# Values of two key steps in one go behind every second step, in a causal two-softmax attention block

## What is computed

```python
scores = einsum('bhid,bhjd->bhij', q, k) / sqrt(hd)
std_out = out_proj(softmax(where(mask, scores, neg)))
gsa_scores = scores + position_sensitivity * splat_attn
gsa_out = out_proj(softmax(where(mask, gsa_scores, neg)))
return (1.0 - blend) * std_out + blend * gsa_out
# the layer
x = layernorm(x + attn(x)); x = layernorm(x + ffn(x))
```

## Time and profile before

| | us |
|---|---|
| median of 3 runs | 417.15 |
| lowest, highest | 415.52, 419.78 |
| the profiled execution | 420.38 |
| its span | 418.6 |

### The profile page before, as it was taken

The page is one execution under the profiler, slowest core; times in us unless marked ns, Lnnn a source line. Parts: engine busy times, 40 slices in busy tenths (PEclk is TensorE's granted clock), DMA queues, the critical chain, the costliest instruction groups (busy, mean ns, idle before and its releaser), DMA issues.

```text
span 418.6 us, 6705 instructions
## 1 busy us (share of the span) xinstructions
PE 392.4 (94%) x2234; PEld 258.5 (62%) x2234; DVE 314.3 (75%) x908; ACT 231.1 (55%) x451; POOL 112.0 (27%) x163
## 2 busy tenths in 40 slices
PE   8989886899999999999999999999887999999995
PEld 7656553566566566566565565556344578888884
DVE  2767744999979889889889789799302447999956
ACT  4964123156666667567567577677486756344100
POOL 8569100020221230230330320346557110000000
PEclk9999978699999999999999999999898999999999
DMA  6152664000044044053053056500000000000002
GB/s 201 36 99 45 102 103 74 1 3 2 3 78 78 4 78 76 6 89 65 6 96 59 7 97 144 215 2 1 3 2 0 2 2 0 0 1 2 2 0 100
DMA packets 12907, 19.69 MB, mean 47 GB/s; under 512 B 5493, under 2 KB 8565, under 8 KB 12873
## 3 DMA queue, kind: packets, MB, share of 16 engines
q1 hardware_dynamic: 10328, 18.18, 21.6%
q0 software_dynamic: 1536, 1.07, 1.5%
q10 hardware_dynamic: 1008, 0.02, 0.1%
HBM read 5.26 MB, written 1.05 MB: 15 GB/s over the span
## 4 chain that ended last, share of the span: by engine, by line
PE 80%; DVE 10%; ACT 6%; issue 2%; DMA 2%; SPq 1%; DVEq 0%; ACTq 0%
PE ps L931 19%; PE ps L905 17%; PE ps L870 16%; PE ps L834 7%; PE ps L736 5%; PE ps L738 5%; PE ps L737 5%; DVE ps L1225 4%; PE ps L892 2%; DMA x_sb<-_attn_hidden_states_dram 2%; ACT pr L684 1%; PE ps L798 1%; DVE mpart L1218 1%; PE ps L818 1%; ACT gauss L643 1%
## 5 line engine op out<-in xcount | busy, mean ns | idle before, releaser
L684 ACT ACTIVATE pr<-ps 128x512 f32<-128x512 f32 (+2 forms) x320 | 157.3, 561 | 82.3 <-PE ps L931 80.8
L1225 DVE CUSTOM_DVE_ANT_0 ps<-ps,causal 128x512 f32<-128x512 f32 (+3 forms) x256 | 145.6, 615 | 15.6 <-PE ps L870 13.8
L870 PE MATMUL ps<-k_st,q_st 65*128 65x512 f32 (+5 forms) x384 | 121.2, 368 | 9.9 <-DVE mpart L1225 6.4
L931 PE MATMUL ps<-q_st,k_st 67*128 67x512 f32 (+7 forms) x384 | 127.1, 374 | 0.0
L931 PEld LDWEIGHTS ps<-q_st,k_st 67*128 67x128 f32 (+1 forms) x384 | 68.4, 191 | 67.8 <-ACT pr L684 42.8
L870 PEld LDWEIGHTS ps<-k_st,q_st 65*128 65x128 f32 (+1 forms) x384 | 69.3, 194 | 26.2 <-DVE mpart L1225 13.7
L905 PE MATMUL ps<-pr,vx 128*32 128x512 f32 (+3 forms) x768 | 83.4, 507 | 1.1 <-ACT o_sb L670 1.1
L528 POOL TENSOR_SCALAR_AFFINE_SELECT pr<-pr 128x512 f32<-128x512 f32 x64 | 40.5, 633 | 115.2 <-ACT pr L684 115.2
L1218 DVE TENSOR_REDUCE mpart<-ps 128x2 f32<-128x256 f32 (+2 forms) x96 | 54.7, 596 | 6.7 <-PE ps L870 6.7
L1225 DVE DVE_READ_ACCUMULATOR2_ANT mpart<- 128x1 f32 x256 | 36.2, 141 | 0.0
L905 PEld LDWEIGHTS ps<-pr,vx 128*32 128x32 f32 x768 | 15.3, 108 | 23.6 <-ACT pr L684 14.6
(11 more groups left out here) (186 smaller groups left out, 511.6 us busy)
## 6 DMA issues: line engine op xcount, KB each, us to landing
q_st<-base_hiq SPq DMA_DIRECT2D x28, 64.0 KB
k_st<-base_hik SPq DMA_DIRECT2D x28, 64.0 KB
q_st<-feat_hiq SPq DMA_DIRECT2D x28, 64.0 KB
k_st<-feat_hik SPq DMA_DIRECT2D x28, 64.0 KB
x_sb<-_attn_hidden_states_dram SPq DMA_DIRECT2D x4, 256.0 KB, 5.8
raw<-in_L_ffn_w_gate_dram SPq DMA_DIRECT2D x1, 1024.0 KB, 4.9
raw<-in_L_ffn_w_up_dram SPq DMA_DIRECT2D x1, 1024.0 KB, 7.1
wd<-in_L_ffn_w_down_dram SPq DMA_DIRECT2D x1, 1024.0 KB, 9.3
```

The costliest lines, as they stand in the source:

```text
L684: act.activation(pr[:, s % NP, 2 * hh + vs[0]:2 * hh + vs[-1] + 1, d:BANK], src, ACT.Exp, scale=SCALE).then_inc(exp_done, 1)
L870: mm = pe.matmul(ps[:, slot, at:at + n], q_st[b][0:rows, hh, i * P:(i + 1) * P], k_st[b][0:rows, hh, first:first + n], start=(v == v0), st ...
L931: mm = pe.matmul(ps[:, bank, j * width:(j + 1) * width], k_st[b][0:rows, hh, kt * P:(kt + 1) * P], q_st[b][0:rows, hh, q:q + width], start ...
L1225: ins = dve.tensor_tensor_reduce(out=ps[:, slot, at:at + n], in0=ps[:, slot, at:at + n], in1=causal[:, BANK - n:BANK], scale=1.0, scalar=- ...
```

## The change

Behind the scores of an odd step PE now does the values of two steps, s - 3 and s - 2, one after the other; behind an even step it does none. The first values come at step 3, the last two steps' behind the loop as before.

The turn of a pair's first half moves from step kt = 2 to kt = 3 of the second half. In the last pair `at` moves from kt = 3 to 4, `wo` from 4 to 5, the square root from 5 to 6; `yt` stays at 7.

```diff
-        if g == 1 and kt == 2:
+        if g == 1 and kt == 3:
             here.append(("turn_out", p, 0))
         if p == PAIRS - 1 and g == 1:
 
-            here += {3: [("at", 0), ("at", 1)], 4: [("wo", 0), ("wo", 1)], 7: [("yt", 0), ("yt", 1)]}.get(kt, [])
+            here += {4: [("at", 0), ("at", 1)], 5: [("wo", 0), ("wo", 1)], 7: [("yt", 0), ("yt", 1)]}.get(kt, [])
...
-                if p == PAIRS - 1 and g == 1 and kt == 5:
+                if p == PAIRS - 1 and g == 1 and kt == 6:
                     deviation(act, 1, slice(0, TPG))
...
-                if s >= PV_LAG:
+                if s % 2 == 1 and s >= PV_LAG + 1:
+                    values(s - PV_LAG - 1)
                     values(s - PV_LAG)
```

## The result

The median went from 418.0 us to 421.03 us (13 runs each, taken in turn); the ratio is 1.0073, with a 95% interval of 1.0045 to 1.010. So the change makes the kernel slower by 3.0 us (1.9 to 4.2), 0.7% and clear of noise. The prediction had 0.6 us more, 417.8, in a range whose upper end was 421.2; the measured time lies 0.2 us inside it.

The account below looks back on a forecast made before the run. PE was taken to set the pace for seven pairs, waits between PE, ACT and DVE in the last. Span 418.6 - 1.6 - 0.2 + 1.5 + 0.9 = 419.2, 0.6 more; median 417.15 + 0.6 = 417.8 us, range 412.8 to 421.2.

Parts of the forecast that it names:

- a switch: PE going between whole-array scores and 32-column values: 0.28 us each, bounds 0.19 and 0.34, 47 fewer.
- steps 54/55: Turn and row matmuls come nearer to DVE's backlog and wait for banks: saved 0.
- steps 56/57: Turn and next two row matmuls wait for DVE's banks, then both value steps follow: 0.83 us lost.
- a pair: Twelve steps such as 48 to 59: gains 0.22 us, not the 1.7 of six switches.
- steps 0 to 79: Start through pair 6 up to step 80: 1.9 us gained in all.
- last pair, clock held: From step 84 on at full clock: yt at 29.7 us instead of 30.5, 0.2 us gained in all.
- the clock, last pair: Half clock behind longer idle stretches: 1.5 us lost behind the one before yt, 0.9 at wo.
- The bank waits: Row matmuls wait until DVE has read the maximum four before; moved values remove its catch-up time, so 54/55 saves 0, 56/57 loses 0.83.
- The end of pair 6: Values of step 78 come behind the wait for the last rows, no longer hidden: 0.27 us lost together.
- Rival A: Switches count, DVE has room: all 47 give 404 us, the half case 412 to 413; chance 0.22.
- Rival B: Half clock decides in four stretches (behind 89 and 91, wo, yt) at 1.5 us each: 421.35 us; chance 0.18.
- C: Nothing measurable: bank waits and clock give back what switches save; the forecast itself, chance 0.60.

Follow-up runs that it names:

- light pair: Kernel before and changed kernel, each with DVE reading only half of each row maximum's columns: 403.93 us (before) and 398.17 us (changed).
- chosen steps: Kernel before with values in twos only behind steps 1, 3, 5 and 11 of each pair, alone from step 80 on: 411.78 us, ratio 0.984.
- kept busy: Unused transposes added ahead of PE's waits: changed kernel 415.04 us, ratio 0.995 (transposes for wo re-placed); kernel before 417.43 us, ratio 1.000.
- early items: Changed kernel, values in twos throughout, with the last pair's turn, at, wo and square root where they were before: 417.07 us, ratio 0.997.
- the first part alone: Changed kernel up to step 79, with the order of the kernel before from step 80 on: 413.85 us, ratio 0.990.
- the last one: Kernel before with the chosen steps, transposes ahead of the last turn of maxima and turn (7, 0), and values in twos from step 84: 408.76 us, ratio 0.979.

## Why the prediction was nearly right

Taken step by step, in us; stretches from profiles, a minus is a gain.

| step of the sum | predicted | measured |
|---|---|---|
| a switch | 0.28 (0.19 to 0.34) | 0.31 to 0.34 where no bank wait stands (light pair), 0.30 on average in the chosen steps (1.19 / 4) |
| steps 48/49, 50/51, 52/53 | -0.77 | -0.94 |
| steps 54/55 | 0 | -0.01 |
| steps 56/57 | +0.83 | +0.88 |
| steps 58/59 | -0.28 | -0.34 |
| a pair | -0.22 | -0.41 |
| steps 0 to 79 | -1.9 | -2.65 |
| steps 80 to 83, clock held | +0.27 | +0.27 (10.08 against 9.81, kept busy both) |
| last pair, clock held | -0.2 | +0.2 (33.92 against the 33.73 of before); +1.3 (against its 32.59, kept busy) |
| the clock, steps 80 to 83 | 0 | +1.6 (2.6 in the changed kernel less 1.0 in the one before) |
| the clock, last pair | +2.4 | +2.9 in the changed kernel; the one before had 1.1 |

**The switch** was priced 0.05 us low. In the changed kernel two value steps in one go hold PE for 1.86 us where one holds it for 1.00, so the second adds 0.86 (forecast 0.91): nearly all of the 0.15 fixed part goes with the switch, not the 0.09 that I had put. With the 0.19 around it that makes 0.33, which is what undisturbed steps save. That agrees with the rule of the Trainium skill (TensorEngine Tiling (Array Packing), Key Properties) that was weighed, that a change of tiling mode drains the engine.

**The bank waits** were right to 0.05 us for each of the two steps on which all hung, 54/55 and 56/57, and the runs with the light DVE and with the chosen steps show that they are the cause: with less load on DVE the pair falls to 29.18, without the change in these steps to 29.61. A pair gains 0.19 more than forecast, nearly all of it in steps 50/51, 52/53 and 58/59, where no wait came and a switch saved 0.34 to 0.36 instead of 0.28.

**The end of pair 6** is the step that failed. The mechanism, values 78 no longer hidden under the wait for the last rows, came at its price, and the wait fell by 0.26 (from 4.26 to 4.00 us behind the last row matmul; predicted 0.4). But I took the clock to cost there what it did before, one stretch of 3.4 us at half. The idle stretch grew from 1.55 to 2.22 us, since the values of 78 had been in front of it, and half clock lasted 6.83 us, over both value steps and into the scores of steps 82 and 83. I had counted the growth for `yt` and `wo`, and not here, though it is the same move. 1.6 us of the 1.85 lost is that, by the profiles: 2.6 regained here when kept busy, less the 1.0 that the kernel before regained.

**The last pair**: yt was put at 29.7 us after step 84 and came at 31.6 (331.83 - 300.23); `wo` was put at 19.8 and came at 20.4. The 1.3 us between are `wo` at half clock, which held PE for 4.6 us (320.63 to 325.24) instead of 3.2 (323.73 to 326.91 before); in the sum it stands as 0.9. With the clock held, 0.4 us separates the forecast (33.5) from the run (33.92). That it is so little is partly luck: the 33.73 from which the forecast started had a stretch of half clock in it, and against the kernel before kept busy too (32.59) the late items cost 1.3. For the clock 2.4 was forecast and 2.9 measured. The Trainium skill's rule (TensorE: Matmul & The Clock Gate, Part 1), that throttled is the default and activity lifts it, agrees with the half clock behind the three idle stretches, and with its absence where transposes filled them. My reading of it was too wide where I wrote that the values kept PE active in the waits: with values in twos and early items the last pair took 32.66 us. There it was the delay of `at`, `wo` and square root by a step that made the waits long.

**Against the median.** The terms add up to 2.3 us between the profiles (249.9 to 252.2), and the runs show 3.0 with 1.9 to 4.2 as interval. The forecast was 0.6 more, a fifth of it, and even that had help: steps 0 to 79 gained some 0.75 us more than forecast, which hid part of what was missed behind step 80. That the time fell inside the range by 0.2 us is luck in part.

**The rivals.** Rival A had it that all or half of the switches would count; the pair at 30.39 us excludes it. (Its half case, worked out as written, is 417.15 - 6 + 2.4 = 413.6, not 412 to 413.) Rival B had half clock decide, in four stretches with 421.35 us; the time was 421.03. It had two of its places wrong (behind 89 and 91 there was none) and missed the longest, behind the last turn of maxima, but the sign of the result is due to its mechanism: with the clock held the changed kernel is 0.5% faster than the one before (0.992 to 0.998). C, nothing measurable, was my forecast; over 13 runs each the difference is clear of noise.

What stays open: how often each half-clock stretch comes in the kernel before. The mean clocks say that keeping it busy took away some 2 us of half clock on average, where one profile showed 6.8. The opening plays into them, as its half clock differs too: some 20 us in the profile of the kernel before, 24 in that of the same kernel kept busy, 17 in that of the changed one.

## What to carry to other kernels

A switch between whole-array and 32-column matmuls cost PE 0.33 us here wherever nothing else held it, so group them, but look up what each group was covering. Where a ring of banks ties PE to a reader that is nearly as busy, moving work out of a gap only saves if the reader had already given its banks back; walk the ring with the trace's ends, and leave alone the steps that don't have room. Before moving work behind a wait, look at how long PE would then be idle: here half clock in three places cost the changed kernel 5.5 us. And one profile is one execution: look at the mean clocks of all runs before taking its half clock for that of the kernel.

## What was not expected of the hardware

- A few dozen transposes without any use, put in three waits, made the changed kernel some 6 us faster (421.03 to 415.04). With them the granted clock was 1.00 through steps 80 to 95; without them 0.73 and 0.91.
- Idle stretches of PE of 0.74 and 0.89 us had no half clock behind them; one of 1.55 us had 3.4 us of it, and one of 2.22 us had 6.8. In between the length of the idle stretch alone doesn't tell: the same 1.46 us before yt left the clock at 1.00 in one kernel (early items) and had 3.4 us of half clock behind it, from 320.95, in another (the last one). In the run of the first part alone 1.33 us before the last turn of maxima left the clock at 1.00.
- The kernel before took 415.8 us in executions with a mean granted clock of 0.978 or 0.979 and 419.8 in those with 0.967.
- A value step that follows another adds 0.86 us at 512 columns, with no gap for its own waits, though both add into the same PSUM bank (1.86 us for the two).
